# Delta loop of a gated delta-rule kernel: decay rows placed ahead of key taps and state products in odd slots, and four tiles in a loop body in place of two

## The reference, cut to what matters

```
qkvz = layernorm(x) @ W_in                    # q, k, v, z: 16 heads x 64 each
q, k, v = silu(causal_conv4(q, k, v))         # depthwise, 4 taps
beta = sigmoid(b);  g = -A * softplus(a + dt_bias)
q = l2norm(q) / 8;  k = l2norm(k)
for each token t of a sequence:               # S is 64 x 64 per head, S = 0 at the start
    S = S * exp(g[t])
    S = S + k[t] (x) ((v[t] - k[t] @ S) * beta[t])
    y[t] = q[t] @ S
x = x + (rmsnorm(y) * silu(z)) @ W_o
```

## Time and profile before

| | |
|---|---|
| median of 3 runs | 6891.01 us (6883.61 to 6892.95) |
| the profiled execution | 6851.76 us, with a span of 6850.0 us |
| busy share of the span | PE 85%, PEld 64%, DVE 54%, ACT 48%, POOL 37% |
| granted TensorE clock, mean | 0.949 |
| stretch of the delta loop | about 170 us to 4206 us, the first and last `rb` of line 1178 |

### The profile page before, as it was taken

The page is one execution under the profiler, slowest core; times in us unless marked ns, Lnnn a source line. Parts: engine busy times, 40 slices in busy tenths (PEclk is TensorE's granted clock), DMA queues, the critical chain, the costliest instruction groups (busy, mean ns, idle before and its releaser), DMA issues. The chain is left out here.

```text
span 6850.0 us, 187736 instructions
## 1 busy us (share of the span) xinstructions
PE 5835.0 (85%) x67109; PEld 4385.9 (64%) x67110; DVE 3713.1 (54%) x7246; ACT 3295.2 (48%) x7154; POOL 2521.4 (37%) x2359
## 2 busy tenths in 40 slices
PE   5999999999999999999999997775888588886687
PEld 4666666666666666666666665563666466665587
DVE  5555555555555555555555555644444466666434
ACT  2555555555555555555555553151333245553265
POOL 5445445444544544444454443341000100001654
PEclk9999999999999999999999998897999889998598
DMA  3000000000000000000000000021000000000124
GB/s 94 21 21 14 21 21 18 17 21 21 18 17 21 17 18 21 21 14 21 21 18 17 21 19 31 23 58 28 0 0 0 2 1 0 0 0 29 43 61 122
DMA packets 99093, 159.13 MB, mean 23 GB/s; under 512 B 19972, under 2 KB 82244, under 8 KB 96068
## 3 DMA queue, kind: packets, MB, share of 16 engines
q1 hardware_dynamic: 76260, 121.44, 5.9%
q0 software_dynamic: 14080, 26.64, 1.2%
q10 hardware_dynamic: 8320, 4.19, 0.2%
HBM read 118.03 MB, written 104.87 MB: 33 GB/s over the span
## 5 line engine op out<-in xcount | busy, mean ns | idle before, releaser
L789 PE MATMUL bank<-wc,hT 128*128 128x512 f32 x2088 | 1049.6, 618 | 77.9 <-issue 59.2
L955 PE MATMUL bank<-X,kqe 128*128 128x64 f32 x6240 | 774.2, 277 | 75.2 <-DVE rb L1448 54.6
L955 PEld LDWEIGHTS bank<-X,kqe 128*128 128x128 f32 x6240 | 726.4, 192 | 99.2 <-DVE rb L1448 70.1
L1186 ACT ACTIVATE TT<-bank 128x512 bf16<-128x512 f32 x640 | 382.1, 597 | 664.1 <-PE bank L936 661.7
L1488 DVE TENSOR_TENSOR yb<-bank,masks 128x512 bf16<-128x512 f32 x768 | 525.7, 685 | 184.3 <-PE bank L918 177.4
L789 PEld LDWEIGHTS bank<-wc,hT 128*128 128x128 f32 x2088 | 349.7, 191 | 344.2 <-issue 315.9
L1286 POOL TENSOR_TENSOR qa<-qa,qt 128x512 f32<-128x512 f32 x390 | 486.8, 1269 | 34.8 <-POOL qt L1281 34.8
L1427 DVE TENSOR_TENSOR kqe<-bank,ex 128x512 f32<-128x512 f32 x520 | 335.0, 686 | 279.6 <-PE bank L863 279.6
L1141 ACT ACTIVATE ex<-bank,gate_bias_all 128x128 f32<-128x128 f32 x1040 | 289.4, 375 | 405.4 <-DVE kqe L1427 201.9
L1186 ACT ACTIVATE T<-bank 128x512 bf16<-128x512 f32 x640 | 348.7, 595 | 272.6 <-PE bank L929 270.5
L1319 POOL TENSOR_SCALAR_AFFINE_SELECT kqe<-kqe 128x512 f32<-128x512 f32 x260 | 215.0, 827 | 712.0 <-DVE kqe L1427 712.0
(11 more groups left out here) (531 smaller groups left out, 13306.5 us busy)
## 6 DMA issues: line engine op xcount, KB each, us to landing
sent_l0f<-blank_l0f SPq DMA_DIRECT2D x64, 528.0 KB
sent_l1m<-blank_l1m SPq DMA_DIRECT2D x64, 528.0 KB
xin<-sent_l1m SPq DMA_DIRECT2D x139, 66.0 KB, 1.9
taken_l1m<-back_l1m SPq DMA_DIRECT2D x16, 512.0 KB, 8.7
xin<-sent_l0f SPq DMA_DIRECT2D x75, 66.0 KB, 1.9
decay_sums<-decay_rows SPq DMA_DIRECT2D x264, 3.0 KB
cw_stage<-in_L_attn_conv_w_dram SPq DMA_DIRECT2D x4, 1024.0 KB, 5.8
out_dram<-x_sb ACTq DMA_DIRECT2D x8, 512.0 KB, 6.8
```

The costliest lines, as they stand in the source:

```text
L789: mm = pe.matmul(bk[:, :], src[:, j:j + P], w["wc"][:, j, at * 512:(at + 1) * 512], start=(j == 0), stop=(j == TAPS - 1))
L955: mm = pe.matmul(bk[:, i * D0:(i + 1) * D0], lhsT(hh), rhs(hh), start=True, stop=True)
L1186: nc.scalar.activation(dst, bk[:, :].rearrange("p (h a u) -> p h a u", h=8, u=1 << l), ACT.Copy).then_inc(actb.done.sem, 1)
```

## The change

1. PE, odd slot: `decay(0)` and `decay(1)`, which stood at the head of `decayed`, now stand ahead of the first two taps of `k1` and ahead of `ks` and `qs`. Even slots keep their order. The ring's order of uses stays as it was.
2. ACT, every slot: `tanh_of("k0")` now stands ahead of `decay(0)`, `decay(1)` and the two copies of the keys; it stood behind them.
3. All engines: the body holds four slots, two sequences, and runs 16 times. `U = 4` is the number of slots; slots 0 and 2 are even, 1 and 3 odd; buffers are picked by `t % 2`; the counters get the new number of uses in a turn. The total of work is the same.

```diff
+    U = 2 * TPB
+    N = turns * U
...
             def decayed(b, t):
 
                 src = hT[t % TPB]
-                decay(b, t, 0)
-                decay(b, t, 1)
+                if t < 0 or t % 2 == 0:
+                    decay(b, t, 0)
+                    decay(b, t, 1)
                 pe.wait_ge(k_ready.sem, k_ready.at(b, t + 2))
                 turn_heads(b, k2, "k")
-                done = 2 if t == 1 else 0
+                done = 2 if t > 0 and t % 2 == 1 else 0
...
             with pe.Fori(0, turns) as b:
-                for t in range(TPB):
-                    taps(b, hT[t], "v0", 2, 2)
+                for t in range(U):
+                    taps(b, hT[t % 2], "v0", 2, 2)
...
                     turn_squares(b, t)
-                    if t == 1:
-                        taps(b, hT[t], "k1", 0, 2)
+                    if t % 2 == 1:
+                        decay(b, t, 0)
+                        decay(b, t, 1)
+                        taps(b, hT[t % 2], "k1", 0, 2)
                         from_state(b, t, 0, "ks")
                         from_state(b, t, 1, "qs")
                     decayed(b, t)
...
+                tanh_of(b, "k0")
                 decay(0)
                 decay(1)
                 evacuate(b, "k.0", kqT[:, 0:4, 0, :])
                 evacuate(b, "k.1", kqT[:, 4:8, 0, :])
-                tanh_of(b, "k0")
                 act.wait_ge(qs_ready.sem, qs_ready.at(b, 2 * (t + 1) + 2))
...
-        delta_attention(nc, c, {"wc": wc, "wq": wq, "cq": cq, "wz": wz, "wo": wo}, x_all, mr, gates, decay_rows, tiles // TPB, sendings)
+        delta_attention(nc, c, {"wc": wc, "wq": wq, "cq": cq, "wz": wz, "wo": wo}, x_all, mr, gates, decay_rows, tiles // (2 * TPB), sendings)
```

More of the change, by code:

```diff
@@ L563, in at @@
     def at(self, t, name):
-        if t == TPB:
+        if t == len(self.slots):
             return self.ahead + self.per + self.behind.index(name) + 1
-        turn, slot = divmod(t, TPB)
+        turn, slot = divmod(t, len(self.slots))
         return self.ahead + turn * self.per + sum(map(len, self.slots[:slot])) + self.slots[slot].index(name) + 1
@@ L623, in act_slot @@
             names += [f"t.{l}.0", f"t.{l}.1"] + ["h"] * (l == 4)
-            names += [f"tt.{l}.0", "s.0", f"tt.{l}.1", "s.1"] if l == 5 and t == 1 else [f"tt.{l}.0", f"tt.{l}.1"]
+            names += [f"tt.{l}.0", "s.0", f"tt.{l}.1", "s.1"] if l == 5 and t % 2 == 1 else [f"tt.{l}.0", f"tt.{l}.1"]
         names += ["tt.6.0", "tt.6.1"]
@@ L634, in dve_slot @@
         names += ["sqt"]
-        return names + ["ks.0", "ks.1", "qs.0", "qs.1"] * t + DVE_D
+        return names + ["ks.0", "ks.1", "qs.0", "qs.1"] * (t % 2) + DVE_D
     QP = [f"qp.{i}" for i in range(PAIRS // 2)]
@@ L710, in delta_attention @@
         k_ready = signal("k_ready", U)
-        kd_ready = signal("kd_ready", 1)
-        rows_in = [signal(f"decay_rows_in{t}", 16 * NHB) for t in range(U)]
+        kd_ready = signal("kd_ready", U // 2)
+        rows_in = [signal(f"decay_rows_in{t}", 16 * NHB * U // TPB) for t in range(TPB)]
         m_ready = signal("m_ready", NHB * U)
         mb_ready = signal("mb_ready", NHB * U)
-        rhs_ready = signal("rhs_ready", 1)
+        rhs_ready = signal("rhs_ready", U // 2)
         rhsb_ready = signal("rhsb_ready", U)
@@ L928, in join_t @@
                     hh = G * 8 + i
-                    mm = pe.matmul(bk[:, i * HALF:(i + 1) * HALF], TT[t][:, hh, :], yb[:, hh, :], start=True, stop=True)
+                    mm = pe.matmul(bk[:, i * HALF:(i + 1) * HALF], TT[t % 2][:, hh, :], yb[:, hh, :], start=True, stop=True)
                 mm.then_inc(actb.full.sem, 1)
@@ L1019, in _ @@
                     level_zero(b, t, 3)
-                    taps(b, hT[t], "v1", 0, 2)
+                    taps(b, hT[t % 2], "v1", 0, 2)
                     turn_zero(b, t, 2)
@@ L1044, in _ @@
                         if l <= 2:
-                            taps(b, hT[t], "v1", l + 1, 1)
+                            taps(b, hT[t % 2], "v1", l + 1, 1)
                         if l == 4:
@@ L1202, in _ @@
             with act.Fori(0, turns) as b:
-                for t in range(TPB):
+                for t in range(U):
                     right_side(b, t)
                     for g in range(NHB):
-                        evacuate(b, f"tt.0.{g}", TT[t][:, g * HB:(g + 1) * HB, :])
+                        evacuate(b, f"tt.0.{g}", TT[t % 2][:, g * HB:(g + 1) * HB, :])
                     squares_k(b, t)
```

54 lines of the change are left out of this document (26 added, 28 removed).

## The result

The changed kernel takes 6769.07 us (median; 6762.3 to 6772.78) against 6889.48 us (6883.61 to 6892.95): a ratio of 0.9825, 95% interval 0.9808 to 0.9842. The direction and both parts are right; the size is not.

The account below looks back on a forecast made before the run. The loop was taken as bound by PE, busy 116.17 of 126.16 us a pass. Branches 33.3 us plus odd slots 50.9 us gave 84.2 us, so 6891.0 to 6806.8 us, range 6788 to 6858.

Parts of the forecast that it names:

- Both waits that the view named: Waits of PE in the loop: 59.2 us in 31 ahead of taps, 57.3 us in 32 on ACT's queries' copy.
- Two old passes: Loop length: two passes of two slots, 252.3 us, should become one pass of four slots of 247.0 to 248 us.
- The odd slot: Odd slots: Exp and tanh run in ACT's idle time, products start 1.59 us earlier, 32 times, 50.9 us.
- PE's work between L816 and L863 is the same set in another order: Odd slot: PE's reordered work keeps its length, so key transposes still start at 2421.35 and taps end at 2424.10.
- The upper end is the whole wait, 57.3 us: Odd slots: at most PE's whole wait on ACT's queries' copy, 57.3 us, can be won.
- The even slots: Even slots: the tanh ahead of the Exp costs nothing, since products start right behind 3.60 us of taps.
- The branch: Loop's end: PE waits for the body's head to be loaded again; 16 fewer branches at 2.08 us save 33.3 us.
- The clock: PE in one pass of the loop: the granted clock was read as full, 1.00.
- the prediction's figure for the profiled execution: Whole kernel: the profiled execution of 6851.76 us less 84.2 us, so 6767.6 us.
- Its lower end, 6788: Whole kernel: 6891.0 less upper ends 57.3 and 36.3 us gives 6797, and 9 us further for the spread of runs.
- ACT's pause at a branch: Loop's branch: ACT with 610 rows would wait for a load too; starting up to 3.4 us later costs nothing.
- The slower rival: ACT's part of the solve: 48 instruction loads at 2.08 us cost 100 us, giving 6907 us; chance 0.04.

Follow-up runs that it names:

- the four lengths of body: The changed kernel with 2, 4, 8 and 32 slots in a body: loops of 3964.7, 3928.4, 3909.4 and 3895.3 us.
- the first four runs: On one chip: kernel before again, 6888.73 us; changed kernel with two slots, 6811.37; with four slots but without both moves, 6843.25; changed kernel again, 6766.83.

## Why the prediction was wrong, point by point

**Where the time goes: right.** Both waits that the view named were the ones that paid, PE bounds the loop before and after, and DVE, ACT and POOL cover their new delays. That the parts add was right as well. **The size was 36 us short by medians, 24 us of it in the loop.** The largest piece is the odd slot, 11 us; 12 us lie outside of the loop and stay open. Two old passes should have become one of 247.0 to 248 us; by the starts of the right sides four slots apart it is 245.4 (median), and was 252.1. The terms, by the loops of the profiles before and after (108.4 us):

| term | forecast | measured |
|---|---|---|
| odd slots, 32 | 1.59 us each, 50.9 | 1.94 each, 62.1 |
| even slots, 32 | nothing | 0.15 each, 4.8 |
| branches, 16 fewer | 2.08 us each, 33.3 | 2.26 each, 36.2 |
| half clock behind pauses | not named | 5.3, the rest |

The last row is what the others leave, not a measurement. Counted by the slots that hold them, the six stretches before cost 9.8 us and the two after 3.3, which gives 6.5.

**The odd slot.** The step that failed is "PE's work between L816 and L863 is the same set in another order, so the transposes of keys still start at 2421.35". They came earlier: from L816 to L830 it takes 2486.74 - 2479.75 = 6.99 us, and took 2421.35 - 2414.09 = 7.26. The same matmuls in another order are 0.27 us shorter. It is PE's move that does it: the way is 6.97 us with that move alone and 7.26 with ACT's alone, and 6.99 with the banks between `ks` and `qs`. The 0.27 us are spread over several groups (among them the taps 1.82 to 1.71 us and the state's products 3.93 to 3.86, from start to start); why these get shorter is open. The other 0.08 us are ACT's queries' copy, which takes 0.63 us now and took 0.71. That sums to 1.94. With it fell "The upper end is the whole wait, 57.3 us": 62.1 us were won where the view showed 57.3.

**The even slots.** The step was "The tanh ahead of the Exp in the even slots costs nothing: there the products start right behind 3.60 us of taps". It costs nothing, but it gains. The queries' copy ended 0.13 us ahead of the products in every slot before, even ones too: PE stood by ACT there, and what looked like "right behind the taps" (0.08 us) was a tie, in which the modelled end of the taps hid a wait. After the change the copy ends 0.38 us ahead in the even slots. The run with ACT's move alone shows this 0.15 us by itself.

**The branch.** Its mechanism was right, its price 9% low. I had added the mean wait and one overlap, 2.08 us. From the medians of the slots' lengths a branch costs 2.26 us before and 2.27 after (between profiles 2.1 to 2.4), and the four lengths of body give 2.3 to 2.4 with the clock's part in it. What the sum left out is small and in two places: the first tap to the solve takes 2.24 us at a branch and 2.17 elsewhere, and the rest of a slot behind a branch is 0.1 us longer. That the pass of the earlier trace rows said 2.27 is luck: its wait of 2.11 us is among the longest of the 31, whose mean is 1.91.

**The clock.** The prediction read 1.00 in one pass and took it for the loop. With PE pausing for 1.6 to 2.2 us twice a pass, some pauses of 1.8 to 2.2 us are followed by 3.4 us at 1.2 GHz: six and seven in the two profiles of before, eight in each of the two runs with one move, three and five with both moves in two slots, five with four slots and no moves, and two, none and one in the three of the changed kernel. None stood behind the odd slot's wait once PE's move had shortened it; behind branches the count went up as well as down (three in one profile of before, eight with one move) while all 31 stayed. So with fewer long pauses there were fewer stretches, but how many an execution gets varies by one or two with the same program, and the 5 us of the table are in part that. Which pauses are followed by such a stretch isn't settled. They come at regular distances in places: by the clock record, the five of the run with four slots and no moves stand 751 us apart, three passes of its loop, and three in the profile of before 505 us, four passes.

**Outside of the loop.** The medians differ by 120 us, the loops by 108 to 110. The two profiled executions differ by less, 6850.0 - 6760.5 = 89.5 us, since behind the last right side the one of before needs 2645 us and the one of after 2663. So it is luck that the prediction's figure for the profiled execution, 6767.6 us, lies only 5 us above the measured 6762.3. On the chip of the first four runs the part behind the loop was 6 us shorter in the changed kernel than in the kernel before, on the third chip it was 2 us shorter than with two slots, and with 32 slots 4 us longer than with two. What sets this is open.

**The range.** Its lower end, 6788, took the two waits of the view as the most that could be won. That is the error that the runs show: a wait in the view bounds neither the gain of an order nor that of a clock. The loop's 108.4 us alone would have given 6783 us, 5 below the range; the other 14 us of the miss are the 12 outside of the loop and the base of the medians, 6889.5 with one more run in place of 6891.0.

**The rivals.** ACT's pause at a branch was named, with its cover of 3.4 us, and it came: 2.60 us, where none was before, with 610 rows in the body in place of 308. PE's first solve isn't held up by it: at every branch without half clock it follows the first tap by 2.24 us, as before the change (2442.40 - 2440.16 in the earlier trace rows), and a branch costs PE nearly the same with ACT's pause (2.2 to 2.4 us) as without (2.1 to 2.3). It is the length of the body that brings the pause, not the moves: the run with four slots and no moves has it 15 times too, 37.0 us on ACT and 58.4 on POOL. ACT's pause agrees with the Trainium skill, Runtime: NRT & Kernel Launch, "Instruction fetch mechanics", by which a taken branch waits where its target is not held any more. POOL paused with a body of 181 rows, and the 512 instructions that the prediction took from that section don't account for it. The slower rival, loads that stand in ACT's part of the solve, did not come: the view of ACT's waits shows pauses without a releaser 15 times, at the branches alone.

```profile
ACT rb L1181 <- issue: 35.4, 15, 2.6
```

The instruction queues changed as well. In the DMA view over the loop, before and after (packets, MB, share):

```profile
q8 instruction: 382, 6.26, 0.7%
q14 instruction: 5, 0.04, 0.0%
```
```profile
q8 instruction: 366, 6.00, 0.7%
q14 instruction: 267, 2.19, 0.2%
```

The queue that had 12 packets in each of 32 passes has 23 in each of 16, and a second one that was nearly silent now moves 17 a pass. The second goes with the length of the body: over the loop it has 5 packets with both moves in two slots, and 267 with four slots and no moves. That its packets are the streams of ACT and POOL, loaded anew in each pass, fits their pauses, but was not shown by itself.

## What to carry to other kernels

When two engines hand work over in a fixed order, look not only at who waits now but at which ends tie: in the even slots PE stood by ACT by a tenth of a microsecond, which no view of waits lists, and a row of such ties over 32 slots is worth some microseconds. A helper's work (here Exp and tanh) wants to start while its engine idles, and how early didn't matter here once it was out of the way of the next copy. A branch of the loop costs PE 2.1 to 2.4 us here, whatever the length of the body, so with the same code a body of 32 slots in place of 4 won another 29 to 34 us, and each pause of about 2 us that goes may take a stretch of half clock with it.

## What the runs showed of the hardware that was not expected

- A pause of PE of 1.8 to 2.1 us in a loop in which PE is 92% busy can be followed by 3.4 us at the lower clock; it happened behind 6 of the 63 pauses of 1.6 to 2.2 us in the profile of before, and in no profile inside the loop without such a pause close ahead.
- POOL paused at the branch for 4.08 us (3.8 on the mean of 15) though its body has 181 rows, longer than ACT (2.60 us) with 610; with 92 rows it had no such pause. With 8 slots its pause is up to 2.8 us. The reason wasn't looked for.
- The same program, the kernel before, differed by 34 us between two profiled executions: the loop by 1.4 us, the part behind it by 34, and 29 us of that in one wait of a stage that the change doesn't touch.
